# Row-maximum scores from the keys' high part alone, on alternating halves of the 128 partitions

## Chip, cores and metric

The kernel runs on one core of one Trainium2 chip. The metric is the time on the device in microseconds (us); lower is better. Of the kernel before, three runs are shown: median 1868.85 us, from 1866.58 to 1869.12.

## What is computed

Tokens x of shape (2, 4096, 512) are normalised, and the output is x + attention(xn) + experts(xn). The attention compresses every token to 64 numbers (C = 64), forms queries, keys and values of 64 numbers with a rotary embedding, and is causal with softmax over up to 4096 keys:

```python
scores = jnp.einsum('btd,bsd->bts', q, k) * scale
scores = jnp.where(causal[None], scores, jnp.float32(-1e+30))
attn = jax.nn.softmax(scores, axis=-1)
o = jnp.einsum('bts,bsd->btd', attn, v)
out = z @ W_to_kv + z @ W_out_res.T + b_out_res      # z = o @ W_comp2lat.T
```

The second part is a mixture of 16 experts of which each token takes two, plus a shared expert.

## The kernel before

The program has three stages, one after the other. `prepare` (to about 765 us of the span) normalises, runs the shared expert, and writes queries, keys, values and the routed token lists to memory. `routed` (765 to about 1524 us) runs the experts and, woven into them, the largest score of every query row. `attend` (from about 1526 us) makes the attention with these maxima and adds everything up.

A number in full precision is held as two parts of the matmul's number format, a high part and the remainder, the low part. A product of two such numbers is three matmuls (`parts`, L64: high x high, high x low, low x high).

`routed` goes through 143 tiles of 128 tokens (`TILES`), one tile in a **slot**. TensorE's program for slot t is written out by hand (L1126 to L1150): `gate_up(t)`, 12 matmuls into `egu`; `down(t - 1)`, 6 matmuls into `edb`; then the maximum scores of the slot, `max_scores` (L1089), into `emb`; then `turn(t + 2)`, four transposes of 128 columns into `etb`; then `turn_hidden(t)`, two transposes into `ehb`. All of these use 128 contraction rows.

The maximum scores are 288 **units** (`unit`, L993), spread evenly over the 129 slots from 6 to 134 (`maxima_until`, L928): 99 slots hold two units and 30 hold three. A unit takes 128 queries and one block c of 512 keys: one matmul whose stationary operand is `qh` (the queries' high part, the same 64 numbers on the lower and on the upper 64 partitions) and whose moving operand is `khl` (the keys' high part on the lower 64 partitions, their low part on the upper). Its 128 contraction rows so give q_high x (k_high + k_low). If the block is the queries' own (64 units), it is cut to 128, 256, 384 or 512 keys, and a second matmul of 128 columns in bf16 adds the causal mask (L1099). Units alternate between two PSUM banks (`mb[g % 2]`), and VectorE reduces each to its largest value (`reduce_max`, L1288). From a slot's third unit on, TensorE waits until the unit two before it has been reduced (L1093). The blocks of one set of 128 queries follow each other in rising c.

The parts come from ScalarE and VectorE some slots ahead. ScalarE loads a group of 512 keys twice into `ka`, on both halves (L1182), and copies it as high part to all 128 partitions of `khl` (`split_high`, L1187, which counts `highs`). VectorE then overwrites the upper half with the low part (`split_low`, L1278, which counts `k_low`). TensorE waits for both at the first unit of a group (L1086, L1087). `attend` uses `khl` again with all its 128 rows, as stationary operand (L1491), against `qh`.

Two places are used for comparison. In slots 136, 137 and 138 `fold_weights` (L1108) puts one small product in the place behind `turn`: a plain fp32 product, run in two passes, with 128 contraction rows and 64 stationary columns (L1112), with 64 and 64 (L1116), and with 64 and 128 (L1119). Ahead of the first of them, also behind `turn`, stands one transpose with 64 stationary columns (L1106). At the program's start, L458 is a plain fp32 product with 128 rows and 128 columns, and transposes follow it (L395).

Of the kernel before, what the change touches and what calls it, by code (L numbers as in the profile page):

```python
# [28 lines left out]
ALU = mybir.AluOpType  # L29
# [3 lines left out]
P = 128  # L33
B, T, D = 2, 4096, 512
N = B * T
E, FE, FS = 16, 256, 512
C = 64
LAT = 128
GT = 4
GROUP = GT * P  # L40
# [10 lines left out]
QB = T // GROUP  # L51
# [7 lines left out]
def value(ap):  # L59

    return ap.bitcast(F32)
# [11 lines left out]
def after(eng, sem, value):  # L73

    if isinstance(value, int) and value <= 0:
        return
    eng.wait_ge(sem, value)
# [847 lines left out]
FIRST_SLOT, LAST_SLOT = 6, TILES - 9  # L925


def maxima_until(t):  # L928


    done = -(-FIRST_MAX[NG] * (t + 1 - FIRST_SLOT) // (LAST_SLOT + 1 - FIRST_SLOT))
    return min(FIRST_MAX[NG], max(0, done))


def routed(nc, res, ew_d, xn_d, parts_d, ident, table, upto_tiles, ids_all, rows_all, w_tiles, q_d, k_d, v_d, max_d,
           khl, kh1, vhl, mop, queries, masks, w_kv, w_c2l, w_outT, tri_in, w_vT, gamma, beta, fold_in,
           w, rows, rows_in, w_in, stored, st_base, base_d, base, base_in):
    with ExitStack() as ctx:
# [12 lines left out]
        ka = [sb(f"ka_{i}", [P, GROUP]) for i in range(2)]  # L951
# [6 lines left out]
        tb, gu, mb = [[ps(f"e{n}{i}") for i in range(2)] for n in ("tb", "gu", "mb")]  # L958
# [9 lines left out]
        highs, k_low, v_low, q_seen = sem("highs"), sem("k_low"), sem("v_low"), sem("q_seen")  # L968
# [9 lines left out]

        group_of = [n for n in range(NG) for _ in range(GT * KEY_GROUPS[n])]
        slot_of = [next(t for t in range(TILES) if maxima_until(t) > FIRST_MAX[n]) for n in range(NG)]  # L980
        split_slot, later = {}, TILES
        for n, which in ((n, which) for n in range(NG - 1, 0, -1) for which in range(3, -1, -1)):
# [4 lines left out]
        def maxima(t):  # L987


            done, until = maxima_until(t - 1), maxima_until(t)  # L990
            return range(done, until)

        def unit(g):  # L993


            n = group_of[g]
            j, c = divmod(g - FIRST_MAX[n], KEY_GROUPS[n])
            return n, j, c, (GROUP if c < n % QB else P * (j + 1))
# [37 lines left out]
        def _(pe):  # L1036
# [43 lines left out]
            def maxima_ready(t):  # L1080

                units = maxima(t)
                if units:
                    after(pe, m_red, units[0])
                for n in (n for n in range(NG) if FIRST_MAX[n] in units):
                    pe.wait_ge(highs, 4 * n + 2)  # L1086
                    pe.wait_ge(k_low, n + 1)  # L1087

            def max_scores(g, t):  # L1089

                n, j, c, width = unit(g)
                if g - maxima(t)[0] > 1:
                    pe.wait_ge(m_red, g - 1)  # L1093
                own = c == n % QB
                key = n // QB * T + c * GROUP
                mm = pe.matmul(mb[g % 2][:, 0:width], qh[n % 3][:, j * P:(j + 1) * P], khl[:, key:key + width],  # L1096
                               start=True, stop=not own)
                if own:
                    mm = pe.matmul(mb[g % 2][:, width - P:width], identb[:, :], future[:, :], start=False, stop=True)  # L1099
                mm.then_inc(m_done, 1)  # L1100
# [25 lines left out]
            for t in range(TILES):  # L1126
                find_buffer()
                gate_up(t)
                if t + 1 < TILES:
                    find_weights(t + 1)  # L1130
                if t > 0:
                    pe.wait_ge(hT_lo, t)
                    after(pe, d_ev, t if t > 1 else 0)
                if t + 2 < TILES:
                    turn_ready(t + 2)
                if t == FIRST_SLOT:
                    pe.wait_ge(bias_ready, 1)
                maxima_ready(t)
                if t > 0:
                    down(t - 1)  # L1140
                pe.reg_mov(last_buffer, this_buffer)
                for g in maxima(t):
                    max_scores(g, t)
                if t + 2 < TILES:
                    turn(t + 2)
                if t == LAST_SLOT + 2:
                    turn_lowest()
                if FOLD <= t < FOLD + 3:
                    fold_weights(t - FOLD)
                turn_hidden(t)  # L1150
# [110 lines left out]
        @block.vector  # L1261
        def _(dve):
            def turned(t):
                dve.wait_ge(t_hi, t + 1)
                dve.tensor_tensor(rT[t % 2][1][:, :, :], tb[t % 2][:, :].rearrange("p (k t) -> p k t", k=KD),  # L1265
                                  value(rT[t % 2][0][:, :, :]), ALU.subtract).then_inc(t_lo, 1)

            def hidden(t):
                dve.wait_ge(sg_done, t + 1)
                after(dve, hb_done, t - 1)  # L1270
                dve.tensor_tensor(h[t % 2][:, :], gu[t % 2][:, FE:2 * FE], sg[t % 2][:, :], ALU.mult).then_inc(h_done, 1)  # L1271

            def hidden_turned(t):
                dve.wait_ge(hT_hi, t + 1)
                dve.tensor_tensor(hT[t % 2][1][:, :, :], hb[:, 0:FE].rearrange("p (k t) -> p k t", k=FK),
                                  value(hT[t % 2][0][:, :, :]), ALU.subtract).then_inc(hT_lo, 1)

            def split_low(n, which):  # L1278
                q, at = n % 2, slice(n * GROUP, (n + 1) * GROUP)
                if which == 0:  # L1280
                    dve.wait_ge(highs, 4 * n + 1)
                    dve.tensor_tensor(khl[C:P, at], ka[q][C:P, :], value(khl[C:P, at]), ALU.subtract).then_inc(k_low, 1)
                if which == 3:
                    dve.wait_ge(highs, 4 * n + 4)
                    dve.tensor_tensor(vhl[:, n, :, C:2 * C], va[q][:, :, :], value(vhl[:, n, :, 0:C]),
                                      ALU.subtract).then_inc(v_low, 1)

            def reduce_max(g):  # L1288

                n, j, c, width = unit(g)  # L1290
                dve.wait_ge(m_done, g + 1)
                if g == FIRST_MAX[n]:
                    after(dve, low_done, n - 1)
                dve.tensor_reduce(mx[n % 2][:, j, c:c + 1], mb[g % 2][:, 0:width], AX.X, ALU.max).then_inc(m_red, 1)  # L1294
                if g + 1 == FIRST_MAX[n + 1]:
                    dve.wait_ge(m_red, g + 1)
                    dve.tensor_reduce(lowest[:, GT * n:GT * n + GT], mx[n % 2][:, :, 0:KEY_GROUPS[n]], AX.X, ALU.max,
                                      negate=True).then_inc(low_done, 1)

            def fold_inputs():  # L1300
                dve.wait_ge(const_in, CONSTS)
                dve.tensor_tensor(wz, wz, wo, ALU.add).then_inc(sum_w, 1)
                dve.tensor_scalar(fold[:, 0, :], fold[:, 0, :], gam[:, 0:1], None, ALU.mult).then_inc(fold_ev, 1)
                dve.wait_ge(fold_ev, 1)
                dve.tensor_copy(fold[:, 0, C - 1:C], bet[:, :]).then_inc(fold_ev, 1)
                dve.wait_ge(fold_ev, 2)
                dve.tensor_copy(fold[:, 1, :], fold[:, 0, :]).then_inc(fold_ev, 1)

            def folded_low():
                dve.wait_ge(mo_ev, 3)  # L1310
                dve.tensor_tensor(mop[1][:, :], mo2, value(mop[0][:, :]), ALU.subtract).then_inc(mo_ev, 1)

            for q in range(2):
                i = dve.memset(value(qlm[q][C:P, :]), 0.0)
            i.then_inc(q_blank, 1)
            turned(0)
            turned(1)
            for t in range(TILES):
                hidden(t)
                if t == 1:  # L1320
                    dve.tensor_copy(identb[:, :], ident[:, :])
                    dve.wait_ge(tri_done, 16)
                    dve.tensor_copy(future[:, :], tri[:, :]).then_inc(bias_ready, 1)
                if t == 3:
                    split_low(0, 0)
                    split_low(0, 3)
                for g in maxima(t):
                    reduce_max(g)
                if t + 2 < TILES:
                    turned(t + 2)  # L1330
                for n, which in splits[t]:
                    split_low(n, which)
                hidden_turned(t)
                if t == FOLD_LOAD + 2:
                    fold_inputs()
                if t == FOLD + 3:
                    folded_low()
            for k in range(2):
                dve.wait_ge(q_split, k + 1)
                dve.tensor_tensor(qlm[k][0:C, :], qa[k][0:C, :], value(qh[k][0:C, :]), ALU.subtract)  # L1340
# [341 lines left out]
```

## Time and profile before

| | before |
|---|---|
| median of three runs | 1868.85 us |
| the profiled execution's own time | 1869.81 us |
| its span, first to last instruction | 1868.0 us |
| mean granted clock of TensorE | 0.985 of full speed |
| TensorE busy | 1761.7 us (94%) |
| VectorE, ScalarE, GpSimd busy | 1147.2, 751.9, 689.3 us |

A row of a timeline gives the start, the time from its start to its end, the engine and line, what is written from what, the stationary operand's rows*columns, the shape of the moving operand, and how many instructions of that kind are merged in it. Matmuls overlap: one of 512 columns is shown as 0.39 us long, but the next starts 0.23 us after it. PEld is the load of a stationary operand, which normally runs while the matmul before it streams.

### The profile page before, as it was taken

The page shows a single profiled execution, that of the slowest core. Times are in us where ns is not written, and L with a number is a line of the kernel's source. Part 1 is how long each engine was busy: PE and PEld are TensorE (multiplying, and loading weights), DVE is VectorE, ACT ScalarE, POOL GpSimd, SP SyncE. Part 2 cuts the span into 40 slices and gives each one's busy share as a digit, 9 for nine tenths or more (in the row PEclk, how much of TensorE's full clock was granted, in tenths as well). Part 3 has the DMA queues.
Part 4 walks back from the last instruction along what each step waited for, and adds up shares of the span by engine and source line. Part 5 has one row for each costly group of instructions (what it writes and reads, how often), then busy time and mean ns, then how long its engine had stood idle before and what let it go on. Part 6 is the DMA issues. An engine that isn't in the chain of part 4 may idle for free. (4 is left out here: it accounts for less than half of the span.)

```text
span 1868.0 us, 28098 instructions
## 1 busy us (share of the span) xinstructions
PE 1761.7 (94%) x8509; PEld 1404.2 (75%) x8509; DVE 1147.2 (61%) x2227; ACT 751.9 (40%) x1287; POOL 689.3 (37%) x676
## 2 busy tenths in 40 slices
PE   2799999999999998999999999999999989999998
PEld 1677777777777776777778777777777767777776
DVE  5777767777777653455555555555555436766675
ACT  2322222222222221433333333333333358888885
POOL 0554455545554552333434333333333320111110
PEclk8799999999999999999999999999999999999999
DMA  7666676566567646545554546555445438899896
GB/s 264 219 190 214 217 224 215 195 222 221 188 191 227 207 150 224 165 149 172 174 176 162 174 154 199 176 176 172 162 155 179 161 65 186 192 242 210 204 219 158
DMA packets 149582, 352.59 MB, mean 189 GB/s; under 512 B 19996, under 2 KB 41564, under 8 KB 149472
## 3 DMA queue, kind: packets, MB, share of 16 engines
q1 hardware_dynamic: 96924, 234.59, 37.4%
q0 software_dynamic: 43968, 104.91, 22.0%
q10 hardware_dynamic: 8580, 11.64, 2.2%
q8 instruction: 67, 1.10, 0.2%
q14 instruction: 43, 0.35, 0.1%
HBM read 208.30 MB, written 146.70 MB: 190 GB/s over the span
## 5 line engine op out<-in xcount | busy, mean ns | idle before, releaser
L1351 POOL DMA_INDIRECT expert_rows<-res,ids_all x143 | 149.7, 1047 | 456.6 <-ACT res L1175 447.4
L1294 DVE TENSOR_REDUCE mx<-emb 128x1 f32<-128x512 f32 (+3 forms) x288 | 175.1, 642 | 108.4 <-PE emb L1096 86.5
L69 PE MATMUL egu<-w,rT_0h 128*128 x576 | 186.8, 406 | 1.2 <-DVE rT_0l L1265 1.2
L69 PE MATMUL egu<-w,rT_1h 128*128 x568 | 182.4, 402 | 0.0
L903 POOL DMA_INDIRECT token_list<-tok,slot x128 | 125.1, 977 | 151.7 <-DVE slot L670 115.8
L1547 ACT ACTIVATE ex<-sc 128x1024 f32<-128x1024 f32 (+4 forms) x176 | 144.9, 823 | 57.8 <-PE sc L1492 50.1
L1271 DVE TENSOR_TENSOR eh<-egu,esg 128x256 f32<-128x256 f32 x143 | 60.7, 424 | 174.3 <-ACT esg L1165 174.3
L1346 POOL DMA_INDIRECT rows<-xn_scratch,rows_all x137 | 132.5, 967 | 47.6 <-issue 43.1
L1612 POOL DMA_DIRECT2D base<-expert_rows x32 | 41.3, 1527 | 265.4 <-DMA base<-base_scratch 244.8
L1165 ACT ACTIVATE esg<-egu 128x256 f32<-128x256 f32 x143 | 54.9, 384 | 187.8 <-PE egu L69 184.9
L1491 PE MATMUL sc<-qh,khl 128*128 128x512 f32 (+3 forms) x288 | 112.9, 392 | 9.0 <-DVE last L1592 2.5
L69 PEld LDWEIGHTS egu<-w,rT_0h 128*128 128x128 f32 x576 | 103.9, 190 | 20.2 <-issue 1.6
L502 ACT ACTIVATE sg<-gb 128x512 f32<-128x512 f32 x64 | 38.2, 597 | 192.2 <-PE gb L69 192.2
L69 PEld LDWEIGHTS egu<-w,rT_1h 128*128 128x128 f32 x568 | 101.5, 189 | 18.3 <-issue 0.4
L69 PE MATMUL gb<-wd_h,h_h 128*128 128x512 f32 x256 | 107.9, 421 | 6.9 <-DVE h_l L691 6.9
L69 PE MATMUL egu<-w,rT_0l 128*128 x288 | 113.9, 395 | 0.0
L1160 ACT CAST rT_0h<-etb 128x512 fp32r<-128x512 f32 x72 | 42.2, 586 | 172.5 <-PE etb L1055 163.5
L69 PE MATMUL egu<-w,rT_1l 128*128 x284 | 111.3, 392 | 0.0
L867 POOL TENSOR_TENSOR xb<-x,bias 128x512 f32<-128x512 f32 x64 | 110.3, 1752 | 0.0
L1492 PE MATMUL sc<-qlm,kh 128*128 128x512 f32 (+3 forms) x288 | 109.6, 381 | 0.0
L1096 PE MATMUL emb<-khl,qh 128*128 128x512 f32 (+3 forms) x288 | 92.7, 391 | 15.5 <-DVE mx L1294 15.2
L1160 ACT CAST rT_1h<-etb 128x512 fp32r<-128x512 f32 x71 | 41.6, 586 | 154.1 <-PE etb L1055 145.2
(285 smaller groups left out, 4652.5 us busy)
## 6 DMA issues: line engine op xcount, KB each, us to landing
w<-expert_parts SPq DMA_DIRECT2D x64, 768.0 KB, 8.3
base<-expert_rows POOLq DMA_DIRECT2D x32, 1024.0 KB, 13.3
expert_parts<-ew_h SPq DMA_DIRECT2D x32, 768.0 KB, 3.5
expert_parts<-ew_l SPq DMA_DIRECT2D x32, 768.0 KB, 5.9
x<-x SPq DMA_DIRECT2D x16, 1024.0 KB, 6.3
xn_scratch<-xn SPq DMA_DIRECT2D x16, 1024.0 KB, 6.6
base_scratch<-xb SPq DMA_DIRECT2D x16, 1024.0 KB, 7.4
base<-base_scratch SPq DMA_DIRECT2D x16, 1024.0 KB, 8.0
```

The source lines that it names most:

```text
L69: mm = pe.matmul(dst, w, m, start=(first and i == 0), stop=(last and i == len(terms) - 1))
L867: i = pool.tensor_tensor(xb4[q][:, j, :], x4[q][:, j, :], bias[:, :], ALU.add)
L903: pool.indirect_dma_start(list_d[:, :], bass.IndirectOffsetOnAxis(ap=slot[q][:, j, c:c + 1], axis=0), tok[q][:, j, c, :], None).then_inc(s ...
L1096: mm = pe.matmul(mb[g % 2][:, 0:width], qh[n % 3][:, j * P:(j + 1) * P], khl[:, key:key + width], start=True, stop=not own)
L1160: act.copy(rT[t % 2][0][:, :, :], tb[t % 2][:, :].rearrange("p (k t) -> p k t", k=KD)).then_inc(t_hi, 1)
L1271: dve.tensor_tensor(h[t % 2][:, :], gu[t % 2][:, FE:2 * FE], sg[t % 2][:, :], ALU.mult).then_inc(h_done, 1)
L1294: dve.tensor_reduce(mx[n % 2][:, j, c:c + 1], mb[g % 2][:, 0:width], AX.X, ALU.max).then_inc(m_red, 1)
L1346: pool.indirect_dma_start(rows[:, t % AHEAD, :], None, xn_d[:, :], bass.IndirectOffsetOnAxis(ap=rows_all[:, t:t + 1], axis=0)).then_inc(ro ...
L1351: pool.indirect_dma_start(parts_d[:, :], bass.IndirectOffsetOnAxis(ap=ids_all[:, t:t + 1], axis=0), res[t % 2][:, :], None, bounds_check=2 ...
L1491: pe.matmul(dst, khl[:, key], qh[k % NQ][:, to:GROUP], start=True, stop=False)
L1492: mm = pe.matmul(dst, kh1[:, key], qlm[k % NQ][:, to:GROUP], start=False, stop=own < 0)
L1547: e = act.activation(dst[:, span(i)], sc[i % 2][:, span(i)], ACT.Exp, scale=SCALE)
```

## The change

- The matmul of a maximum score takes 64 contraction rows: the lower half of the partitions for an even key block c, the upper half for an odd one. It multiplies the queries' high part by the keys' high part alone, and the low part leaves the maxima. (The maxima are an offset in the softmax, which divides out; the scores of `attend` keep both parts.)
- So `khl` has to hold the high part on the half that is read: for even key groups the low part stays on the upper half, for odd groups it goes to the lower half. The same instruction writes it, on other partitions.
- The wait for `k_low` before the first unit of a group goes.

The numbers of instructions on every engine and their order stay as they were. The mask matmul (L1099) keeps its 128 rows.

```diff
+def high_rows(n):
+    return slice(n % 2 * C, n % 2 * C + C)
...
                 for n in (n for n in range(NG) if FIRST_MAX[n] in units):
                     pe.wait_ge(highs, 4 * n + 2)
-                    pe.wait_ge(k_low, n + 1)
...
                 own = c == n % QB
-                key = n // QB * T + c * GROUP
-                mm = pe.matmul(mb[g % 2][:, 0:width], qh[n % 3][:, j * P:(j + 1) * P], khl[:, key:key + width],
+                key, high = n // QB * T + c * GROUP, high_rows(c)
+                mm = pe.matmul(mb[g % 2][:, 0:width], qh[n % 3][high, j * P:(j + 1) * P], khl[high, key:key + width],
                                start=True, stop=not own)
...
                 if which == 0:
                     dve.wait_ge(highs, 4 * n + 1)
-                    dve.tensor_tensor(khl[C:P, at], ka[q][C:P, :], value(khl[C:P, at]), ALU.subtract).then_inc(k_low, 1)
+                    low = high_rows(n + 1)
+                    dve.tensor_tensor(khl[low, at], ka[q][low, :], value(khl[low, at]), ALU.subtract).then_inc(k_low, 1)
```

## Rows read from the trace of the kernel before

**Rows 1.** The page, busy time of each engine, its share and instructions:
```profile
PE 1761.7 (94%) x8509; PEld 1404.2 (75%) x8509; DVE 1147.2 (61%) x2227; ACT 751.9 (40%) x1287; POOL 689.3 (37%) x676
```

**Rows 2.** The slots with units as one stretch: length, busy by engine, PEclk, DMA share:
```profile
765.00:1485.00 720.00, 700.08 (x3462) 566.34 (x3461) 391.25 (x726) 261.76 (x576) 276.53 (x289) 1.00 0.50 172
```

**Rows 3.** Waits of TensorE in that stretch: total us, times, longest:
```profile
PE emb L1096 <- DVE mx L1294: 15.2, 28, 0.6
```

**Rows 4.** Timeline, matmuls, one slot with two ordinary units:
```profile
983.46 0.39 PE L69 MATMUL edb<-w,hT_0l 128*128 x1
983.68 0.62 PE L1096 MATMUL emb<-khl,qh 128*128 128x512 f32 x2
984.14 0.60 PE L1055 MATMUL etb<-ident,rows 128*128 128x128 f32 x4
984.58 0.38 PE L1077 MATMUL ehb<-ident,eh 128*128 128x128 f32 x2
984.71 0.48 PE L69 MATMUL egu<-w,rT_0h 128*128 x1
```

**Rows 5.** Timeline, weight loads of the same slot:
```profile
983.46 0.41 PEld L1096 LDWEIGHTS emb<-khl,qh 128*128 128x128 f32 x2
983.91 0.59 PEld L1055 LDWEIGHTS etb<-ident,rows 128*128 128x128 f32 x4
```

**Rows 6.** Timeline, matmuls, slot 137 from its fourth transpose:
```profile
1494.89 0.27 PE L1055 MATMUL etb<-ident,rows 128*128 128x128 f32 x1
1495.09 0.43 PE L1116 MATMUL emb<-fold,wv 64*64 64x128 f32 x2
1495.45 0.44 PE L1077 MATMUL ehb<-ident,eh 128*128 128x128 f32 x2
1495.65 0.48 PE L69 MATMUL egu<-w,rT_0h 128*128 x1
```

**Rows 7.** Timeline, weight loads of slot 137:
```profile
1495.09 0.19 PEld L1116 LDWEIGHTS emb<-fold,wv 64*64 64x64 f32 x2 [0.17 <-issue]
1495.45 0.20 PEld L1077 LDWEIGHTS ehb<-ident,eh 128*128 128x128 f32 x2 [0.17 <-issue]
```

**Rows 8.** Timeline, matmuls, slot 138 from its fourth transpose:
```profile
1500.19 0.27 PE L1055 MATMUL etb<-ident,rows 128*128 128x128 f32 x1
1500.39 1.12 PE L1119 MATMUL emb<-qa,fold 64*128 64x512 f32 x2
1501.45 0.44 PE L1077 MATMUL ehb<-ident,eh 128*128 128x128 f32 x2
```

**Rows 9.** By line, L1119's two matmuls: shortest/median/longest in ns:
```profile
L1119 PE MATMUL emb<-qa,fold x2: 589/641/693, 1500.4 to 1500.9; 64*128 64x512 f32 x2
```

**Rows 10.** Timeline, matmuls, from a plain product with 128 rows to transposes:
```profile
15.52 0.63 PE L458 MATMUL nb<-wcT,ht 128*128 128x64 f32 x2
15.95 0.42 PE L395 MATMUL tb<-ident,xn 128*128 128x128 f32 x1
```

**Rows 11.** Timeline, weight loads there:
```profile
15.73 0.44 PEld L395 LDWEIGHTS tb<-ident,xn 128*128 128x128 f32 x2
```

**Rows 12.** Timeline, matmuls, slot 136, two steps with 64 stationary columns:
```profile
1488.95 0.27 PE L1106 MATMUL emb<-ident,lowest 128*64 128x128 f32 x1
1489.15 0.64 PE L1112 MATMUL emb<-ka,wc 128*64 128x512 f32 x1
```

**Rows 13.** Timeline, matmuls, a slot whose first unit is an own block:
```profile
988.93 0.22 PE L1096 MATMUL emb<-khl,qh 128*128 128x128 f32 x1
988.99 0.23 PE L1099 MATMUL emb<-future,identb 128*128 128x128 bf16 x1
989.03 0.48 PE L1096 MATMUL emb<-khl,qh 128*128 128x512 f32 x1
989.35 0.27 PE L1055 MATMUL etb<-ident,rows 128*128 128x128 f32 x1
```

**Rows 14.** Timeline, matmuls, a slot with three units:
```profile
1004.58 0.50 PE L1096 MATMUL emb<-khl,qh 128*128 128x512 f32 x2
1004.93 0.23 PE L1099 MATMUL emb<-future,identb 128*128 128x128 bf16 x1
1005.76 0.50 PE L1096 MATMUL emb<-khl,qh 128*128 128x512 f32 x1 [0.60 <-DVE mx L1294]
```

## The prediction

> **What bounds the kernel now.** I read the page first: TensorE is busy for 94% of the span, and no other engine for more than 61% [rows 1]. Next the stretch in which the changed matmuls stand: in 720 us TensorE is busy for 700, at a granted clock of 1.00 (the 2.4 GHz level), with the DMA engines half used [rows 2]. Its waits there are 15.2 us in 28 places, all at a maximum score that waits for a reduction [rows 3]. So any time that TensorE gains or loses inside a slot is gained or lost at the end. Then the timeline of one slot: five rows that follow each other without a hole, and every load of weights starts together with the matmul ahead of it (983.46 and 983.46, 983.91 for the transposes, ahead of 984.14), so loads are hidden [rows 4, 5]. Two 512-column matmuls in a row start 0.23 us apart (983.68 to 984.14 are two such steps) [rows 4]. The columns alone take 512 / 2.4 GHz = 0.213 us.
>
> **What halving the rows does not buy.** Time goes by columns. The number of columns of every unit stays, so a 64-row matmul that runs by itself costs the same 0.23 us. The wait on k_low that goes costs nothing now: TensorE's only waits on VectorE at these matmuls are those for the reductions [rows 3]. VectorE's subtraction is the same instruction on another half; I cost it at nothing, since VectorE is busy for 391 of 720 us there [rows 2] and TensorE no longer waits for it. `attend` sums the same 128 products in another order: nothing.
>
> **What going from 128 rows to 64 and back costs.** The kernel before does this in two slots, in the very place of interest. In slot 137 the fourth transpose starts at 1494.89; its columns take 0.11 us (four transposes in 984.14 to 984.58). Yet the load of the 64-row product starts only at 1495.09, 0.20 after the transpose's start, or 0.09 after its last column, instead of together with it [rows 6, 7]. On the way back the same: second pass from 1495.25, 0.11 of columns, load of the next transpose at 1495.45, again 0.09 late [rows 6, 7]. As the load started late, it is also not hidden. Its price is in the first matmul behind it: L1119's first pass is shown 0.104 us longer than its second [rows 9], the first transpose on the way back about 0.06 longer than in an ordinary slot (0.44 against 0.38 for the two) [rows 4, 6]. Slot 138 repeats it: load 0.20 after the transpose, the way back 0.44 [rows 8]. The sum agrees with the whole slot: from the fourth transpose to the first of ehb, 1494.89 to 1495.45, plus 0.06, is 0.62 against 0.11 in an ordinary slot and 0.21 of columns of its own: 0.30 us lost on one visit to 64 rows; in slot 138, with 128 columns of weights, 0.35.
>
> Is it the rows, or that these are plain fp32 products? A plain product with 128 rows and columns hands over to transposes with the load at 15.73, 0.00 after the matmul's start (15.52 + 0.63 - 0.42) [rows 10, 11]. So it is not the plain product as such. One pair speaks against so simple a rule: between L1106 and L1112, both shown as 128*64, there is the same 0.20 step [rows 12]. I leave a chance to that below. The Trainium skill says in "TensorEngine Tiling (Array Packing)", Key Properties, that a change of tiling mode, not of tile alone, drains TensorE; it gives no price. By that rule, the trace agrees at 64 rows with 0.09 us each way; the mode would change on every slot here.
>
> **The sum.**
> - Way in, 129 slots: 0.09 late, 0.104 load, less the 0.013 by which an ordinary step is longer than its columns: 0.184 x 129 = 23.7 us.
> - Way out into transposes, the 99 slots whose last unit has no mask: 0.09 + 0.06 - 0.02 = 0.13 x 99 = 12.9 us.
> - Way out into the mask (128 rows, already unhidden now: 988.93 to 988.99 is the 128 columns alone [rows 13]), the 30 slots whose last unit is an own block: 0.09 x 30 = 2.7 us.
> - An own block that is not the slot's last: out for the mask and in again. 34 of these; 14 stand in slots of three units, where the third waits for a reduction anyway (0.60 us idle [rows 14]) and hides it. The other 20: 0.09 out; and in, 0.053 + 0.09 + 0.107 = 0.25 where 0.04 + 0.09 = 0.13 goes now (989.03, shown 0.09 longer than an ordinary matmul [rows 13]): 0.22 x 20 = 4.3 us.
> - Together 43.6 us.
> - Back: neighbouring units of opposite parity stand on disjoint rows and in different banks, and could run at once. In two-unit slots there are 79 such pairs with no mask between (in three-unit slots the third unit's wait hides any gain). No row shows two matmuls at once. Bounds per pair: nothing, or the whole step of 0.227 (17.9 us). I take what the loads leave: both come after the stall, one after the other at 0.107 each, so the second matmul starts 0.107 behind the first in place of 0.227: 0.12 x 79 = 9.5 us. That is nearer the middle than either end, because the loads' pace is the one thing rows show.
> - Net +34.1 us.
>
> Against the profiled execution's own time: 1869.81 + 34.1 = 1903.9. That execution lies 0.96 above the median of the runs, so the **prediction is 1903 us**, 1.8% slower.
>
> The unknown costs: a visit to 64 rows was 0.30 and 0.35 us in the two slots, less 0.03 of ordinary spacing; I used 0.31 for the common slot. With 0.27 the 43.6 becomes about 38, with 10% more, 48. With the two ends of the overlap: 38 - 18 = +20 to +48, or 1889 to 1917.
>
> **Rivals.**
> 1. *No overlap at all* (the pairs run one after another, each with its 0.227): the change does not do what alternating halves suggest. +43.6: 1912.5. For: no row shows an overlap. Against: nothing but the absence. Chance 0.25.
> 2. *Full overlap*: both matmuls of a pair run together. The Trainium skill ("TensorE: Matmul & The Clock Gate", Part 3) has matmuls in different row groups start 4 ns apart and weights of another row group load beside a running matmul. In rows: 79 x 0.227 = 17.9 back, +25.7: 1894.6. Against: the loads come unhidden here, behind each stall. Chance 0.15.
> 3. *Faster: no stall.* If what held slots 136 to 138 up was something else about the fold products (a plain product of several passes next to transposes with 64 columns, as L1106 to L1112 hints), the 512-column matmuls at 64 rows follow the others at 0.227, and only the overlap is left: -9.5 to -17.9, or 1851 to 1859. It decides below 0.07 us per visit, where 129 visits cost less than the 9.5. For: [rows 12]. Against: [rows 10, 11], and that the 0.09 is the same in L1116 and L1119, into and out of the 64 rows. Chance 0.11.
> 4. *Neither*: no stall and no overlap, 1869 within 0.2%. Chance 0.03.
>
> **Numbers.** My case holds 0.40, rivals 1 and 2 0.40 together, and 0.06 is left for a stall of another size, such as one side only (about +15 to +20, 1887). A measurement of this kernel can tell about 0.2% (3.7 us) from no change. Slower by more: 0.86; within: 0.03; faster: 0.11. The range is that of the slow cases with their bounds, 1887 to 1917; what it leaves out is rivals 3 and 4 and the edges of the 0.06.
>
> **What would show it.** The timeline of an ordinary slot: the load of the first emb matmul starting about 0.30 after the last edb matmul's start instead of with it, that matmul shown 0.10 longer, and the first load of etb starting 0.30 after the last emb matmul. Step from the first egu matmul of a slot to that of the next: about 0.2 to 0.3 us more than before, in every slot with units, and unchanged in the slots before 6, in `prepare` and in `attend`. The two units of a pair about 0.11 apart; 0.23 apart is rival 1, near 0 is rival 2. TensorE's waits on reductions stay at about 15 us, its clock in the stretch at 1.00. If the stretch of 765 to 1485 grows by less than 10 us, or the loads still start with the matmul ahead, the reasoning is wrong; if the time comes from `attend` or from waits on VectorE, it is wrong as well.

## The result and the profile after

The changed kernel takes 1893.45 us (median of four runs, 1892.23 to 1899.14) against 1867.71 us for the kernel before (four runs): 1.0144 of it, 95% interval 1.0121 to 1.0167 (ratios here and below are of the means of the runs, times are medians). It is 25.7 us slower by the medians. The forecast was 34 us slower, 1903 us, and its range of 1887 to 1917 us holds the result. The profiled execution took 1893.85 us.

The page of the changed kernel, busy time by engine:

```profile
PE 1781.6 (94%) x8509; PEld 1377.7 (73%) x8509; DVE 1143.2 (60%) x2227; ACT 751.9 (40%) x1287; POOL 687.9 (36%) x676
```

The same instructions, and TensorE still busy 94% of the span, as in [rows 1]. Where the time went shows in the line of the maximum scores. It gives shortest/median/longest in ns, then the starts of the first and the last, in us. First the kernel before, then the changed one:

```profile
L1096 PE MATMUL emb<-khl,qh x288: 220/389/507, 765.8 to 1478.7; 128*128 128x512 f32 x128, 128*128 128x128 f32 x8, 128*128 128x384 f32 x8
```

```profile
L1101 PE MATMUL emb<-khl,qh x288: 323/497/504, 763.0 to 1503.4; 64*128 64x512 f32 x128, 64*128 64x128 f32 x8, 64*128 64x384 f32 x8
```

The time from the start of the first unit to the start of the last, called **the stage** below, has grown from 712.9 to 740.4 us, by 27.5, and its median matmul is shown 0.108 us longer. The first unit starts 2.8 us earlier than before; that belongs to the preparation. The two make 24.7 us, and the two profiled executions differ by 24.0. The stretch that holds the stage, by engine, and TensorE's waits in it (to compare with [rows 2, 3]; the stretch is 26 us longer than there):

```profile
765.00:1511.00 746.00, 723.44 (x3452) 542.07 (x3451) 386.72 (x724) 262.46 (x576) 275.55 (x288) 1.00 0.48 165
```

```profile
PE emb L1101 <- DVE mx L1300: 19.2, 28, 0.8
```

The granted clock is 1.00, as before, and the waits are still 28, with 4 us more. The forecast had them stay at about 15 us; where the 4 us come from is shown by the first experiment. Then one slot with two ordinary units of opposite parity, matmuls and weight loads, the counterpart of [rows 4, 5]:

```profile
1269.78 0.39 PE L69 MATMUL edb<-w,hT_0l 128*128 x1
1270.10 0.49 PE L1101 MATMUL emb<-khl,qh 64*128 64x512 f32 x2
1270.53 0.66 PE L1061 MATMUL etb<-ident,rows 128*128 128x128 f32 x4
1271.02 0.38 PE L1083 MATMUL ehb<-ident,eh 128*128 128x128 f32 x2
```

```profile
1270.10 0.19 PEld L1101 LDWEIGHTS emb<-khl,qh 64*128 64x128 f32 x2 [0.35 <-issue]
1270.52 0.42 PEld L1061 LDWEIGHTS etb<-ident,rows 128*128 128x128 f32 x4 [0.24 <-issue]
```

Three things are in these rows. The load of the first unit starts 0.32 us after the last edb matmul, about 0.10 after its 0.213 of columns (the median of the 60 plain slots of two units is 0.103), where it used to start with it. The load of the transposes starts 0.42 after the units: 0.107 of load, 0.213 of columns and 0.10 of stall. And the two units, matmuls and loads alike, are one row each: 0.49 us for both matmuls, the length of one, and 0.19 for both loads, also the length of one. They run at the same time, loads included. So a slot that took 0.68 from the edb matmul to the transposes [rows 4] takes 0.75, and the first transpose is shown 0.06 longer.

In a slot whose first unit is an own block the mask brings TensorE back to 128 rows in between:

```profile
902.88 0.39 PE L69 MATMUL edb<-w,hT_1l 128*128 x1
903.19 0.44 PE L1101 MATMUL emb<-khl,qh 64*128 64x384 f32 x1
903.57 0.23 PE L1104 MATMUL emb<-future,identb 128*128 128x128 bf16 x1
903.73 0.49 PE L1101 MATMUL emb<-khl,qh 64*128 64x512 f32 x1
```

The mask starts 0.38 after the unit, whose 384 columns are 0.160 and whose load is 0.107: 0.11 of stall. The next unit starts 0.16 after the mask, whose columns take 0.053: 0.11 again. Its load is not hidden either: it is shown as 0.49, against the 0.39 of a 512-column matmul whose load is hidden.

Going through all slots by kind gives the whole picture (median time in us from a slot's first egu matmul to the next slot's, computed from the traces; an own block is the one with the mask):

| kind of slot | slots | before | after | on one half | pairs only |
|---|---|---|---|---|---|
| two units, opposite parity, no own block | 60 | 5.24 | 5.34 | 5.56 | 5.35 |
| two units, the second an own block, opposite | 19 | 5.32 | 5.36 | 5.52 | 5.28 |
| two units, the first an own block | 20 | 5.24 to 5.37 | 5.83 to 5.91 | 5.80 to 5.91 | 5.26 to 5.34 |
| three units | 30 | 6.29 to 6.30 | 6.57 to 6.63 | 6.57 to 6.62 | 6.27 to 6.29 |

(The last two columns are experiments below: all units on one half, and 64 rows in some slots only.)

### The profile page after: what moved, and what is told of

It is laid out like the page before. It is cut to its first block and busy times, and to the rows that moved or that the text cites. A ratio compares the mean times of both kernels' runs of the same rounds, so it can differ in the third digit from the quotient of the medians.

```text
span 1891.4 us, 28098 instructions
## 1 busy us (share of the span) xinstructions
PE 1781.6 (94%) x8509; PEld 1377.7 (73%) x8509; DVE 1143.2 (60%) x2227; ACT 751.9 (40%) x1287; POOL 687.9 (36%) x676
## 5 line engine op out<-in xcount | busy, mean ns | idle before, releaser
L69 PEld LDWEIGHTS egu<-w,rT_1h 128*128 128x128 f32 x568 | 101.6, 189 | 17.9 <-issue 0.4
L1101 PE MATMUL emb<-khl,qh 64*128 64x512 f32 (+3 forms) x288 | 88.5, 477 | 19.2 <-DVE mx L1300 19.2
```

The source lines that it names most:

```text
L69: mm = pe.matmul(dst, w, m, start=(first and i == 0), stop=(last and i == len(terms) - 1))
L1101: mm = pe.matmul(mb[g % 2][:, 0:width], qh[n % 3][high, j * P:(j + 1) * P], khl[high, key:key + width], start=True, stop=not own)
```

## The experiments

My theory after this: a change between 128 and 64 contraction rows stalls TensorE by 0.10 us each way and leaves the next load unhidden; disjoint halves give a whole matmul back where two units follow each other. Rivals: that halves or overlap do not matter, that the stall belongs to the place or to something else of these products, and that the wait that went hides a gain. There were twelve runs, of ten new kernels; in two runs a kernel that had already run was run again. They ran on several chips, and the kernel before took 1867, 1874 and 1886 us on them (medians). In the traces the preparation differs: the first unit starts between 763 and 784 us. The stage is steady: two traces of the changed kernel show it within 0.5 us. So I read both the ratio to the kernel before on the same chip and the stage. Stages are differences of starts that are shown to 0.1 us. The kernel before has one trace, so its stage is always 712.9.

**All units on the lower half**, in the changed kernel:

```diff
-    return slice(n % 2 * C, n % 2 * C + C)
+    return slice(0, C)
...
-                    low = high_rows(n + 1)
+                    low = slice(C, P)
```

> The changed kernel with all its 64-row matmuls on the lower half of the partitions (the low part of the keys always on the upper half). Theory: a visit to 64 rows costs about 0.33 us in every slot whichever half is used, and what the alternating halves give back is that the 79 neighbouring units of opposite parity in slots of two run at once; on one half they run one after the other, so the time is 79 x 0.225 = 17.8 us above the changed kernel: about 1911 us, and the second emb matmul of a slot starts 0.23 us after the first in place of 0.00. Rival, that the halves do not matter and the price of the change is all there is: 1893 us, as the changed kernel. Rival, that using the upper half is itself what costs: below 1893 us.

Measured: 1917.19 us, 1.0238 (1.0206 to 1.0271) of the kernel before, where the changed kernel was 1.0144. Matmuls of an ordinary slot, and the stage:

```profile
1263.69 0.40 PE L69 MATMUL edb<-w,hT_0l 128*128 x1
1264.02 0.73 PE L1101 MATMUL emb<-khl,qh 64*128 64x512 f32 x2
1264.68 0.55 PE L1061 MATMUL etb<-ident,rows 128*128 128x128 f32 x3
```

```profile
L1101 PE MATMUL emb<-khl,qh x288: 217/492/502, 771.9 to 1527.0; 64*128 64x512 f32 x128, 64*128 64x128 f32 x8, 64*128 64x384 f32 x8
```

Two units take 0.73 in place of 0.49. The way in is the same (0.33), and between two units on the same half there is no stall: the second one's load starts 0.11 after the first one's and is hidden, and the second one starts 0.34 after the first, whose load and columns take 0.107 and 0.213. The stage is 755.1, 14.7 above the changed kernel and 42.2 above the kernel before. So the halves do matter, and what they give is the overlap. I had 0.225 us for each of 79 pairs, 17.8 in all, but two matmuls at once save only the shorter one. In the 60 plain slots that is 0.22 us each. In the 19 slots whose second unit is an own block it goes by that unit's columns: 0.05, 0.11, 0.18 and 0.22 us for 128, 256, 384 and 512 (medians of 7, 5, 3 and 4 slots). That makes 15.6 us; all other slots together are 0.9 us shorter here than in the changed kernel.

The overlap also explains the waits. TensorE's waits for reductions are 13.9 us over the whole stage with all units on one half, and 19.2 us in the changed kernel, 5.3 more. In 25 of the 30 slots of three units the first two run at once, and 25 times 0.22 is 5.5: the third unit waits for the first one's reduction, so it waits longer by what the overlap saved.

**The wait for k_low put back**, in the changed kernel:

```diff
                     pe.wait_ge(highs, 4 * n + 2)
+                    pe.wait_ge(k_low, n + 1)
```

> The changed kernel with the wait for k_low put back before the first unit of each group. Theory: that wait was always over before TensorE came to it, so the time is that of the changed kernel, 1893 us within 0.2%. Rival, that part of the result hides a gain from the wait that went: some us above 1893.

Measured: 1905.91 us, 1.0163 (1.013 to 1.0196). By the median this was 12 us above the changed kernel. But the kernel before took 1874.0 us on that chip, and the stage, 773.1 to 1513.3, was 740.2 against 740.4. To settle it, both ran side by side (the 745.8 and 745.6 us in the next text count the stage from the first egu matmul of slot 6 to that of slot 135):

> The changed kernel itself, beside the next one on the same chip. The stage with the units took 745.8 us in its first trace and 745.6 us with the wait put back, while the preparation ahead of it, which neither touches, took 9 us longer in the run with the wait. Every theory: the stage again 745.7 us; what the preparation takes here shows what belongs to the chip.

> The changed kernel with the wait for k_low put back, again. Theory, that the wait costs nothing: the same median as the changed kernel on this chip, within 0.2%. Rival, that it costs 12 us, as the first medians (1893.5 and 1905.9) have it: 0.6% more.

Measured: 1906.77 us without the wait (1.0119, 1.0094 to 1.0145) and 1909.52 us with it (1.0129, 1.0106 to 1.0153), 0.14% apart; the stages are 739.9 and 739.5. The wait that went was worth nothing that these runs can show, and the 10.5 us between the first two profiled executions stand almost whole in the preparation (first unit at 773.1 against 763.0 us), which neither kernel touches.

**64 rows only where they overlap**: in the changed kernel, with the wait for k_low kept, only slots with exactly two units of opposite parity and no own block (`paired(t)`) take 64 rows.

```diff
-                key, high = n // QB * T + c * GROUP, high_rows(c)
+                key, high = n // QB * T + c * GROUP, high_rows(c) if paired(t) else slice(0, P)
```

> 64 rows only in the 60 slots that hold exactly two units of opposite parity, neither an own block; all other units with 128 rows, as before, and the wait for k_low kept. Theory: each of the 60 visits costs 0.33 us and gives back 0.225, so 60 x 0.105 = +6.3 us against the kernel before: about 1874 us; all other slots as before. Rival, that overlap outweighs the visit when no mask matmul and no third unit stand beside it: 1868 us or less. Rival, that the loss of the change comes evenly from all slots: 60/129 of it, +12 us, 1880 us.

Measured: 1880.23 us against 1874.0, 1.0036 (1.0022 to 1.0051), or +6.7 us; the stage is 720.8, +7.9. The theory's +6.3 lies in the interval, +12 and "not slower" lie outside; summed over the 60 slots alone, the traces differ by 6.3. Even where everything suits it, a visit to 64 rows costs more than the overlap gives back.

**The stall by itself.** Into the kernel before, one more matmul per slot, in 137 slots, between the transposes of turn and turn_hidden, its result unused. Its shape differs between the variants, and in the last two its number format:

```diff
+                if t >= FIRST_SLOT:
+                    pe.matmul(hb[:, 2 * P:4 * P], khl[:, 0:P], khl[:, P:3 * P], start=True, stop=True)
```

with `khl[0:C, ...]` for 64 rows, `hb[0:C, ...]` and `khl[:, 0:C]` for 64 stationary columns, `pe.transpose(hb[0:C, 2 * P:3 * P], ident[:, 0:C], ident[:, :])` for the transpose, and the operands read as plain fp32 in the last two.

> The kernel before with one more matmul in each of the 137 slots from 6 on, between the four transposes of turn and the two of turn_hidden: 128 contraction rows, 128 stationary columns, 256 moving columns, of the keys' parts of group 0, into unused columns of the ehb bank; its result is not used. It is the measure for the next three. Every theory: 256 columns are 0.107 us, the load is hidden beside the transposes, so about 0.13 us x 137 = +18 us, 1886 us, and the added load starts with the matmul ahead of it.

> The same added matmul with 64 contraction rows (lower half). Theory, that the price is for the change of rows alone: a visit costs 0.10 + 0.10 on the way in and 0.10 + 0.06 on the way out, less spacing, about 0.33 us x 137 = +45 us over the kernel with 128 rows: about 1931 us. Rival, that the stall in the changed kernel comes from its place between edb and etb or from two matmuls at once: as with 128 rows, 1886 us.

> The same added matmul with 128 contraction rows and only 64 stationary columns. Theory, that any change of the part of the array that a product takes costs the same stall, columns as rows: about 0.10 + 0.05 in and 0.10 + 0.06 out, about +40 us over 128 x 128: 1926 us. Rival, that only a change of rows stalls: 1886 us; then the step between L1106 and L1112 has another cause.

> In the same place a transpose with 64 stationary columns (64 columns of the identity), as L1106 is. The transpose of L1106 showed no late load behind the 128 x 128 ones, and the product with 64 columns behind it did. Theory, that transposes always take the whole array: no stall on either side, 128 moving columns, about 0.11 us x 137 = +15 us, 1883 us. Rival, that a transpose with 64 columns also changes the part of the array: a late load on at least one side, +0.15 to +0.3 us more each, 1903 us or more.

> The added matmul of 128 x 128 as a plain fp32 product, which runs in two passes of 0.21 us for its 256 columns. Measure for the next one. Theory, that a plain product in itself does not stall: about 0.43 us x 137 = +59 us, no late load. Rival: a load 0.1 us late on either side, +80 us.

> The same plain fp32 product with 64 stationary columns, as L1112 is, behind 128 x 128 transposes. Theory, that a plain product with 64 columns does change the part of the array that is used, while the same in the matmul's own number format (which gave 1881 us, as 128 columns did) does not: loads 0.1 us late on both sides, about +0.25 us x 137 = 35 us over the plain one with 128 columns. Rival, that the step from L1106 to L1112 came from the transpose with 64 columns ahead of it: no late load here, the time of add_plain128.

| added | time, us | ratio to before (95%) | stage, us |
|---|---|---|---|
| nothing | 1866.97 | | 712.9 |
| 128 x 128 | 1881.16 | 1.0078 (1.0061 to 1.0094) | 726.1 |
| 64 rows, 128 columns | 1921.76 | 1.0290 (1.0273 to 1.0307) | 764.5 |
| 128 rows, 64 columns | 1880.97 | 1.0075 (1.0058 to 1.0092) | 725.8 |
| transpose, 64 stationary and 128 moving columns | 1879.46 | 1.0072 (1.0054 to 1.0089) | 723.0 |
| plain fp32, 128 x 128 | 1932.91 | 1.0246 (1.0212 to 1.0280) | 758.6 |
| plain fp32, 64 columns | 1972.16 | 1.0454 (1.0417 to 1.0491) | 796.8 |

The last two are medians of two runs, on a chip on which the kernel before took 1885.79; their ratios are to that. A plain fp32 product takes two passes (x2 in the rows below). Matmuls of one slot with the added 128 rows, and with 64:

```profile
1003.11 0.60 PE L1055 MATMUL etb<-ident,rows 128*128 128x128 f32 x4
1003.46 0.37 PE L1077 MATMUL ehb<-khl 128*128 128x256 f32 x1
1003.67 0.38 PE L1079 MATMUL ehb<-ident,eh 128*128 128x128 f32 x2
```

```profile
1003.50 0.60 PE L1055 MATMUL etb<-ident,rows 128*128 128x128 f32 x4
1004.03 0.38 PE L1077 MATMUL ehb<-khl 64*128 64x256 f32 x1
1004.34 0.44 PE L1079 MATMUL ehb<-ident,eh 128*128 128x128 f32 x2
```

Half the rows and the same columns: start to start 0.53 in place of 0.35 on the way in, 0.31 in place of 0.21 on the way out, and the next transpose 0.06 longer, together 0.34. The median slot is 0.35 longer, near the 0.33 that I had written for this run. But 40.6 us over 137 visits are only 0.296 each, since about a fifth of the slots grew by less than 0.2; what takes the difference up there I have not traced. So 0.30 is the average price of a visit, and neither the place nor the pairing makes the stall.

The columns answer in part what had been left open at [rows 12]. In the matmul's own number format 64 stationary columns cost nothing against 128 (1880.97 and 1881.16), so the expectation of a column stall was wrong there. A transpose with 64 does not stall either: 1879.46, where 1883 was expected without a stall and 1903 or more with one. A plain fp32 product with 128 columns added 47 us, less than the 59 expected without a stall; over all slots its loads start with the matmul ahead. With 64 columns it does stall. Loads of the plain one with 128 columns, then with 64:

```profile
1004.05 0.30 PEld L1077 LDWEIGHTS ehb<-khl 128*128 128x128 f32 x2
1004.38 0.36 PEld L1079 LDWEIGHTS ehb<-ident,eh 128*128 128x128 f32 x2
```

```profile
1000.93 0.19 PEld L1077 LDWEIGHTS ehb<-khl 128*64 128x64 f32 x2 [0.17 <-issue]
1001.51 0.20 PEld L1079 LDWEIGHTS ehb<-ident,eh 128*128 128x128 f32 x2 [0.39 <-issue]
```

With 64 columns the first load starts 0.20 after the last transpose (0.00 with 128), and the next transpose's load 0.31 after the second pass (0.00 with 128; medians of 137 slots). The stage is 38.2 us longer, again 0.30 for each of its visits. So the step between L1106 and L1112 belongs to the plain fp32 product with 64 stationary columns, which stalls against a transpose, and not to the transpose with 64. Why the format decides it, no run here shows; the rows show both as 128*64.

**A version that beats both.** [Rows 3] show that the only waits of TensorE in the stage are those of a third unit. This experiment takes the kernel before, with 128 rows, and puts that unit behind the transposes:

```diff
-                for g in maxima(t):
+                for g in maxima(t)[:2]:
                     max_scores(g, t)
                 if t + 2 < TILES:
                     turn(t + 2)
+                for g in maxima(t)[2:]:
+                    max_scores(g, t)
```

> The kernel before with 128 rows, and one thing moved: in the 30 slots with three units the third one's matmul stands behind the four transposes of turn in place of ahead of them. Theory: TensorE's waits on reductions, 15.2 us in 28 places of about 0.55 us each, are then covered by 0.44 us of transposes, so 28 x 0.44 = 12 us go: about 1856 us, 0.6% faster than before. Rival, that VectorE, which reduces the third unit before it makes the low part of turn's result, now comes late and TensorE waits for it in the next slot: nothing gained, 1868 us, with the waits at edb or egu grown by what the waits at emb lost.

Measured: 1862.19 us against 1874.0 on the same chip, 0.9947 (0.9930 to 0.9965); the stage is 701.9, 11.0 shorter, where 12 had been expected. Compare with [rows 14]:

```profile
1001.18 0.61 PE L1055 MATMUL etb<-ident,rows 128*128 128x128 f32 x4
1001.94 0.50 PE L1096 MATMUL emb<-khl,qh 128*128 128x512 f32 x1 [0.16 <-DVE mx L1296]
1002.28 0.38 PE L1077 MATMUL ehb<-ident,eh 128*128 128x128 f32 x2
```

```profile
PE edb L69 <- DVE hT_0l L1277: 1.5, 3, 0.9
PE edb L69 <- DVE hT_1l L1277: 1.5, 3, 0.6
PE emb L1096 <- DVE mx L1296: 0.5, 3, 0.2
```

The waits at edb in the kernel before (window 765 to 1485):

```profile
PE edb L69 <- DVE hT_0l L1275: 1.7, 3, 0.9
PE edb L69 <- DVE hT_1l L1275: 1.6, 4, 0.7
```

The wait of 0.60 is 0.16 here, and 15.2 us of waits at emb are 0.5. The waits at edb are what they were, so VectorE is not late.

## Why the prediction was right, and where it was off

The time lies in the range, and the costs of the visits were right in kind and nearly in size. What I held most likely for a pair, its two units 0.11 us apart, is not what happened: they start together. Between the forecast and the result lie 8.4 us: 5.2 are that term, 1.4 the visits, and 2.8 a preparation that was shorter though the change does not touch it; 1.0 goes the other way.

- **TensorE bounds the stage, and what is added in a slot arrives at the end.** Right: 27.5 us in the stage, 25.7 us in the time.
- **The way in, 0.09 late and 0.104 of load, 129 times (23.7 us).** Right: 0.10 late and 0.107 of load, in sum as forecast. (The terms as printed there make 0.181, not 0.184, and the 0.22 of an own block in the middle is 0.21; together 0.6 us.) The added 64-row product confirms that a visit, in and out, has a price of its own that comes with the rows alone, 0.296 on average.
- **The way out, 0.13 (12.9 us), and 0.09 into the mask (2.7 us).** Right in kind: 0.10 and 0.06 into transposes, 0.11 into the mask.
- **An own block in the middle costs another 0.22 in a slot of two, and nothing in a slot of three.** Right: 20 slots of two grew by 0.54 to 0.60, where 0.184 + 0.13 + 0.22 = 0.53 was forecast; the 30 slots of three grew by 0.27 to 0.34, whether or not an own block stood in the middle.
- **The sum without overlap, 43.6 us.** Measured with all units on one half: 42.2 us in the stage.
- **The overlap, 0.12 for each of 79 pairs (9.5 us).** This is the term that was mis-sized. I let the two loads come one after the other, 0.107 apart, since rows showed no two loads at once. The trace shows both loads and both matmuls together (x2 in 0.19 and x2 in 0.49). The 60 plain pairs gave back 0.22 each, the other 19 between 0.05 and 0.22; in the stage all slots together 14.7 us. With 14.7 in place of 9.5, 43.6 gives +28.9, against 27.5 measured in the stage. I also gave all 79 pairs the same, while the shorter unit sets what is saved. So rival 2, to which I gave 0.15, described the pairs. That its +25.7 is also the measured difference of the times is partly luck: it has 17.9 back where the rows show 14.7, and the measured time has a preparation that was 2.8 us shorter. The Trainium skill ("TensorE: Matmul & The Clock Gate", Part 3) has loads of another row group run beside a matmul and matmuls of different row groups start 4 ns apart; the trace agrees: it shows one start for both, in rows that resolve 0.01 us.
- **The signs.** The load 0.30 after the last edb matmul, the unit shown 0.10 longer and the clock at 1.00 came as written. The step of a slot did not: forecast were 0.2 to 0.3 us more in every slot with units, and it was 0.10 in the 60 plain ones, 0.04 in the 19 with an own block second, and 0.54 to 0.60 in the 20 with one first. The waits for reductions rose from 15.2 to 19.2 us instead of staying.
- **The removed wait and the moved subtraction cost nothing.** Right for the wait, by two kernels side by side. The subtraction was not tried by itself; TensorE has no wait on it in either trace.
- **Rival 3, faster, because the fold slots' stall was something else.** Wrong: the stall is there in the matmul's own format. What spoke for it, the step at L1106, is a stall of its own, of a plain product with 64 columns, and of the same size.

## What to carry to other kernels

A few 64-row matmuls among 128-row ones are no cheaper than full ones: each visit costs 0.30 us on average and 0.35 in the median slot (a stall of 0.10 each way and a load that is no longer hidden), more than the 0.23 us of one 512-column matmul. Two on opposite halves do run at once and give the shorter one back, 0.22 us for 512 columns, so by these prices a visit would have to hold at least two such pairs with no 128-row product between them (that was not run; here there are two PSUM banks for the units, and each 512-column reduction takes VectorE 0.69 us). Before halving the work of the busiest engine, look for the rows in which it waits: moving one matmul behind four transposes gained 0.5% where this change lost 1.4%.

## What the runs showed that was not expected

- The weight loads of two row halves run at the same time, not only their matmuls: x2 in 0.19 us, the length of one.
- Whether 64 stationary columns stall depends on the number format: nothing in the matmul's own format (1880.97 against 1881.16 us with 128 columns), 0.30 us per visit as plain fp32 (stage 796.8 against 758.6), with the same 128*64 in the rows.
- Two matmuls at once in a slot of three units gained nothing: the third unit's wait grew by the 0.22 us that they saved (13.9 us of waits with one half, 19.2 with both).
- The preparation stage differs from chip to chip and run to run by up to 21 us, nearly the size of the change: first unit at 763 to 784 us, while the stage of the changed kernel was 739.9 to 740.4 us in two traces of it, and 739.5 to 740.2 with the wait put back.
